# Readout at the end of TensorE's scan step, half of a convolution on VectorE, distances stored by token

## The reference

```
u = silu(conv4(u) + conv_b)                       # causal, 4 taps, per channel, per sequence
dt, B, C = split(u @ W_x.T)
delta = softplus(dt @ W_dt.T + b_dt)
for t in 32 tokens:
    h = exp(delta_t * A) * h + (delta_t * u_t) outer B_t
    y_t = sum over the state of h * C_t
out = ((y + u * Dp) * silu(z)) @ W_out.T
```

## Time and profile before

| | us |
|---|---|
| median of 3 runs | 1948.91 (1948.72 to 1953.33) |
| the profiled execution | 1953.92 |
| its span, first to last instruction | 1952.1 |
| TensorE busy | 1711.4 |
| VectorE busy | 1011.8 |
| ScalarE busy | 761.7 |
| GpSimd busy | 703.1 |

### The profile page before, as it was taken

How to read it: one execution, slowest core, us unless ns; L and a number is a source line. 1 busy time by engine, 2 the same in 40 slices (tenths; PEclk the granted TensorE clock), 3 DMA queues, 4 the chain that set the end, 5 groups by cost and what they waited for, 6 DMA issues and landing times.

```text
span 1952.1 us, 24426 instructions
## 1 busy us (share of the span) xinstructions
PE 1711.4 (88%) x9096; PEld 821.3 (42%) x9096; DVE 1011.8 (52%) x1520; ACT 761.7 (39%) x1201; POOL 703.1 (36%) x430
## 2 busy tenths in 40 slices
PE   7888886898999999999997759999812979899998
PEld 4666663542322332332333525444401557644443
DVE  2444444255888888888884333222359464522121
ACT  1333332196676666666661222111413240112121
POOL 0433330215998998998995010000000014000000
PEclk8999997798999999999999768999865879789999
DMA  2111101002000100100100600111062100101110
GB/s 68 32 32 32 32 27 52 0 8 96 12 12 7 29 12 7 29 12 7 29 6 17 223 1 0 33 48 32 5 143 70 33 0 1 44 1 43 44 43 21
DMA packets 36491, 65.63 MB, mean 34 GB/s; under 512 B 13509, under 2 KB 22617, under 8 KB 34981
## 3 DMA queue, kind: packets, MB, share of 16 engines
q1 hardware_dynamic: 33204, 63.42, 11.0%
q10 hardware_dynamic: 3200, 1.07, 0.2%
HBM read 55.80 MB, written 8.67 MB: 33 GB/s over the span
## 4 chain that ended last, share of the span: by engine, by line
PE 80%; DVE 12%; ACT 2%; DMA 2%; issue 2%; POOL 1%; SPq 1%; DVEq 0%; ACTq 0%; POOLq 0%
PE ps L845 17%; PE ps L888 7%; PE ps L1376 6%; PE ps L2123 6%; PE ps L2112 6%; PE ps L860 5%; PE ps L201 4%; PE ps L1389 3%; PE ps L342 3%; PE ps L347 3%; PE ps L224 3%; PE ps L360 2%; DVE arena L477 2%; PE ps L1887 2%; PE ps L1903 2%
## 5 line engine op out<-in xcount | busy, mean ns | idle before, releaser
L1156 POOL TENSOR_TENSOR arena<-arena 128x768 f32<-128x768 f32 x248 | 521.5, 2122 | 75.2 <-DVE arena L1106 45.0
L845 PE MATMUL ps<-arena 32*128 32x512 f32 x2016 | 368.7, 647 | 2.9 <-DMA arena<-m_bd 2.9
L1106 DVE TENSOR_TENSOR arena<-arena,ps 128x1024 f32<-128x1024 f32 x248 | 302.0, 1218 | 11.7 <-POOL arena L1156 5.5
L845 PEld LDWEIGHTS ps<-arena 32*128 32x128 f32 x2016 | 130.0, 184 | 194.2 <-issue 165.2
L1086 DVE TENSOR_TENSOR arena<-arena,ps 128x1024 f32<-128x1024 f32 x124 | 151.4, 1221 | 87.5 <-PE ps L845 87.5
L1012 ACT ACTIVATE arena<-arena 128x1024 f32<-128x1024 f32 x124 | 131.0, 1057 | 166.1 <-DVE arena L1086 166.1
L2069 POOL TENSOR_TENSOR arena<-arena 128x1024 f32<-128x1024 f32 x16 | 29.9, 1896 | 435.0 <-DVE arena L2002 421.7
L888 PE MATMUL ps<-arena 128*32 128x512 f32 (+15 forms) x1024 | 136.2, 604 | 9.4 <-DVE arena L1106 8.9
L1019 ACT ACTIVATE arena<-ps 128x1024 f32<-128x1024 f32 x124 | 127.0, 1024 | 19.7 <-PE ps L845 3.4
L1021 ACT ACTIVATE arena<-arena 128x1024 f32<-128x1024 f32 x124 | 131.1, 1057 | 3.9
L1376 PE MATMUL ps<-arena 128*128 128x512 f32 x288 | 131.8, 602 | 0.6 <-ACT arena L1441 0.6
(11 more groups left out here) (291 smaller groups left out, 2345.3 us busy)
## 6 DMA issues: line engine op xcount, KB each, us to landing
arena<-ctxT SPq DMA_DIRECT2D x32, 257.0 KB, 3.0
arena<-ctxT SPq DMA_DIRECT2D x8, 1028.0 KB, 15.2
arena<-L_ffn_w SPq DMA_DIRECT2D x16, 512.0 KB, 4.3
arena<-ctx_rows SPq DMA_DIRECT2D x8, 960.0 KB
m_rows<-arena SPq DMA_DIRECT2D x16, 256.0 KB, 3.0
arena<-m_rows SPq DMA_DIRECT2D x64, 64.0 KB
arena<-L_ffn_eW SPq DMA_DIRECT2D x8, 512.0 KB, 3.5
m_yd<-arena SPq DMA_DIRECT2D x64, 32.0 KB, 2.3
```

The costliest lines, as they stand in the source:

```text
L845: mm = nc.tensor.matmul(ps[:, bank + jj, :], weights[r], m_row[r, n // CH % 2, n % CH, :], start=start, stop=True)
L1106: nc.vector.tensor_tensor(m_h[:, u, n % 2], m_xa[:, u, n % 2], ps[:, bank:bank + 2, :], ALU.add).then_inc(S["m_use"], 1)
L1156: nc.gpsimd.tensor_tensor(x, x, m_h[:, u, (n - 1) % 2].rearrange("p j d -> p (j d)")[:, own], ALU.mult).then_inc(S["m_kept"], 1)
```

## The change

1. In the scan, `read_out(n - 1)` comes after `logs(n + 2)`, at the end of the step.
2. The convolution of half 1 is taken from TensorE and done by VectorE from `m_xm` into `m_u` (one product and three fused multiply-adds for each channel block), before the silu. Relu also goes to VectorE (`md_pos`), and the order of TensorE and ScalarE ahead of the scan is new: both `steps_and_b` come before both `step_sizes`, `u_by_token(0)` after them; ScalarE has the silus of both halves together, and its exp of half 1 between the squares of half 0. Banks of the spread of C, of the turned B and of the gate products change.
3. `dist` is laid out (token, segment, 87) in place of (segment, token, 87). The store and the three loads of a group stay one transfer each.

```diff
-        dist = nc.dram_tensor("dist", (3, T, 87), F32, kind="Internal").ap()
+        dist = nc.dram_tensor("dist", (T, 3, 87), F32, kind="Internal").ap()
def conv(h):   # on TensorE
-                    if g == 6:
-                        pe.wait_ge(*S.at("m_eaev", 1))
-                    if g == 7:
-                        pe.wait_ge(*S.at("m_alev", 1))
def steps_and_b(h):
-                pe.wait_ge(*S.at("mc_ev_a", IC * h + IC))
+                pe.wait_ge(*S.at("mc_ev_a", 2 * IC - 1 + h))
def u_by_token(h):
-                    pe.wait_ge(*S.at("md_ev", 2 * q + 2))
+                    pe.wait_ge(*S.at("md_ev", q + 1))
+                    pe.wait_ge(*S.at("md_pos", q + 1))
+                    if h and i < 2:
+                        pe.wait_ge(*S.at("m_cev", 2 * i + 2))
+                    if h and i == 2:
+                        pe.wait_ge(*S.at("m_bev", 2))
...
+            steps_and_b(1)
             step_sizes(0)
-            conv(1)
+            pe.wait_ge(*S.at("m_alev", 1))
+            pe.wait_ge(*S.at("m_eaev", 1))
+            step_sizes(1)
             u_by_token(0)
-            steps_and_b(1)
-            step_sizes(1)
...
             for n in range(8):
-                if n == 0:
-                    pe.wait_ge(*S.at("m_dudone", 4))
-                elif n < 3:
-                    pe.wait_ge(*S.at("m_cev", 2 * n))
-                elif n == 3:
-                    pe.wait_ge(*S.at("m_bev", 2))
+                if n < 4:
+                    pe.wait_ge(*S.at("m_dudone", n + 1))
...
             for n in range(STEPS):
                 drive(n, 0)
-                if n:
-                    read_out(n - 1)
                 if rated(n + 2):
                     rates(n + 2)
                 drive(n, 1)
                 if rated(n + 2):
                     logs(n + 2)
+                if n:
+                    read_out(n - 1)
def parts(h):  # on ScalarE
-                    act.wait_ge(*S.at("md_mm", q + 1))
-                    nc.scalar.activation(m_delta[:, q, :], ps[:, bank_of(h, i), :], ACT.Relu).then_inc(S["md_ev"], 1)
+                    act.wait_ge(*S.at("md_pos", q + 1))
                     nc.scalar.activation(m_e[:, q, :], ps[:, bank_of(h, i), :], ACT.Abs).then_inc(S["md_ev"], 1)
...
             for c in range(IC):
                 convolved(0, c)
+                convolved(1, c)
             steps_and_b(0)
             act.wait_ge(*S.at("m_eat", 1))
             nc.scalar.copy(m_EA, ps[:, 6, :]).then_inc(S["m_eaev"], 1)
+            steps_and_b(1)
             parts(0)
+            exponential(0)
             square(0, 0)
             square(0, 1)
-            convolved(1, 0)
+            parts(1)
             square(0, 2)
-            for c in range(1, IC):
-                convolved(1, c)
             square(0, 3)
+            exponential(1)
             square(0, 4)
-            steps_and_b(1)
-            parts(1)
             square(1, 0)
+            spread_c(0)
             square(1, 1)
-            spread_c(0)
-            square(1, 2)
             spread_c(1)
...
+            square(1, 2)
             square(1, 3)
             square(1, 4)
# on VectorE, after the eight copies
+            for c in range(IC):
+                dve.wait_ge(*S.at("mi_ev_d", IC + c + 1))
+                x3, y3 = (half(v, c, 1).rearrange("p (b t) -> p b t", t=L) for v in (m_xm, m_u))
+                ch.link(nc.vector.tensor_scalar(half(m_u, c, 1), half(m_xm, c, 1), m_cw[:, c, KW - 1:KW], None, ALU.mult))
+                for s in range(1, KW):
+                    ins = nc.vector.scalar_tensor_tensor(out=y3[:, :, s:], in0=x3[:, :, :L - s],
+                                                         scalar=m_cw[:, c, KW - 1 - s:KW - s], in1=y3[:, :, s:],
+                                                         op0=ALU.mult, op1=ALU.add)
+                    if s < KW - 1:
+                        ch.link(ins)
+                ins.then_inc(S["m_dconv"], 1)
# and before the products of softplus
+            for q in range(TT):
+                dve.wait_ge(*S.at("md_mm", q + 1))
+                nc.vector.tensor_scalar(m_delta[:, q, :], ps[:, bank_of(q // 4, q % 4), :], 0.0, None,
+                                        ALU.max).then_inc(S["md_pos"], 1)
# distances
-                    sp.dma_start(d_D[r, k:k + L].rearrange("p j i -> p (j i)"),
-                                 dist[k, g * P:(g + 1) * P].rearrange("(b j) i -> b (j i)", j=L)).then_inc(S["d_back"], 16)
+                    sp.dma_start(d_D[r, k:k + L],
+                                 dist[g * P:(g + 1) * P, k].rearrange("(b j) i -> b j i", j=L)).then_inc(S["d_back"], 16)
-                act.dma_start(dist[:, g * P:(g + 1) * P].rearrange("k p i -> p k i"), d_dt[g]).then_inc(S[f"d_out{g % 4}"], 16)
+                act.dma_start(dist[g * P:(g + 1) * P].rearrange("p k i -> p (k i)"), d_dt[g].rearrange("p k i -> p (k i)")).then_inc(S[f"d_out{g % 4}"], 16)
```

More of the change, by code:

```diff
@@ L798, in m_pe @@
             mm.then_inc(S["m_alt"], 1)
+            steps_and_b(1)
             step_sizes(0)
-            conv(1)
+            pe.wait_ge(*S.at("m_alev", 1))
+            pe.wait_ge(*S.at("m_eaev", 1))
+            step_sizes(1)
             u_by_token(0)
-            steps_and_b(1)
-            step_sizes(1)
             for h in range(NH):
-                pe.wait_ge(*S.at("m_dudone", h + 1))
-                spread_c(h, bank_of(0, h))
-            pe.wait_ge(*S.at("m_dudone", 3))
-            pe.wait_ge(*S.at("m_dtev", 4))
[L809 to L813, removed]
+                pe.wait_ge(*S.at("md_ev", 5 + h))
+                pe.wait_ge(*S.at("md_pos", 5 + h))
+                spread_c(h, bank_of(1, h))
+            pe.wait_ge(*S.at("md_ev", 7))
+            pe.wait_ge(*S.at("md_pos", 7))
+            pe.wait_ge(*S.at("m_dtev", 4))
+            for q in range(TT):
+                mm = nc.tensor.transpose(ps[:, bank_of(1, 2), q * NS:(q + 1) * NS], m_Bc[NS:P, q * P:(q + 1) * P],
+                                         ident[NS:P, NS:P])
+            mm.then_inc(S["m_bmm"], 1)
             u_by_token(1)
             for n in range(8):
-                if n == 0:
-                    pe.wait_ge(*S.at("m_dudone", 4))
-                elif n < 3:
-                    pe.wait_ge(*S.at("m_cev", 2 * n))
-                elif n == 3:
-                    pe.wait_ge(*S.at("m_bev", 2))
+                if n < 4:
+                    pe.wait_ge(*S.at("m_dudone", n + 1))
                 else:
                     pe.wait_ge(*S.at("mz_ev", n - 3))
-                product(bank_of(0, (n + 3) % 4), P, [(m_win[:, k, (IC + n % 4) * P:(IC + n % 4 + 1) * P], half(U[2], k, n // 4))
-                                                     for k in range(DC)], "mz_mm")
+                product(bank_of(0, n % 4), P, [(m_win[:, k, (IC + n % 4) * P:(IC + n % 4 + 1) * P], half(U[2], k, n // 4))
+                                               for k in range(DC)], "mz_mm")
             pe.wait_ge(*S.at("mz_ev", 8))
@@ L931, in convolved @@
                 g = IC * h + c
-                act.wait_ge(*S.at("mc_mm", g + 1))
-                nc.scalar.activation(half(m_u, c, h), ps[:, g, :], ACT.Silu,
+                if h == 0:
+                    act.wait_ge(*S.at("mc_mm", c + 1))
+                    src = ps[:, g, :]
+                else:
+                    act.wait_ge(*S.at("m_dconv", c + 1))
+                    src = half(m_u, c, h)
+                nc.scalar.activation(half(m_u, c, h), src, ACT.Silu,
                                      bias=m_cb1[:, c:c + 1]).then_inc(S["mc_ev_a"], 1)
@@ L1006, in m_act @@
                     act.wait_ge(*S.at("mz_mm", 4 * h + i + 1))
-                    nc.scalar.activation(half(m_z, i, h), ps[:, bank_of(0, (i + 3) % 4), :], ACT.Silu).then_inc(S["mz_ev"], 1)
+                    nc.scalar.activation(half(m_z, i, h), ps[:, bank_of(0, i), :], ACT.Silu).then_inc(S["mz_ev"], 1)
             logged(1)
@@ L1144, in m_pool @@
                 pool.wait_ge(*S.at("m_quad", 5 * h + 5))
-                pool.wait_ge(*S.at("md_ev", 8 * h + 8))
+                pool.wait_ge(*S.at("md_pos", 4 * h + 4))
                 for q in range(4 * h, 4 * h + 4):
```

14 lines of the change are left out of this document (8 added, 6 removed).

## The result

The changed kernel takes **2049.24 us** (median of four, 2047.08 to 2055.82) against 1948.90 for the kernel before in the same comparison: ratio 1.0515, 95% interval 1.0486 to 1.0543, +95 to +106 us. The profiled execution took 2048.51 us (span 2046.7), +94.6 in both against that of before. The forecast was 2028, its range ended at 2046: the sign came out, and so did the mechanism of the largest part, but not the size.

What follows compares the result with a forecast made beforehand. It took the mixer's scan as the bound, its 4.57 us step closing over readout, rates and state u=1, with TensorE nearly full. Scan +81, setup -0.7, distances -1 gave +79: median 2028 us, range 2008 to 2046.

Steps and rivals of the forecast that it cites:

- The first link: Scan step, new order: from d0 to VectorE's start on state u=0, 1.18 us of the predicted 5.25 us step.
- Scan: +81 us: Moved readout: +0.68 us in 123 of 128 steps, less 1 us at each of three crossings between groups.
- TensorE's own sum: Scan step, new order: TensorE's work without the new wait on VectorE, put at 4.94 us.
- The first rival: Scan step: TensorE's own sum of 4.94 us decides, the new wait doesn't; +40, 1989 us; chance 0.08.
- The lost neighbours: Scan step: log spread runs alone (1.07 us), d0 beside rates on the same rows (0.94 us), losing their side-by-side overlap.
- my own sum for the old order without waits: Scan step, old order: TensorE's sequence without waits takes 4.12 of the 4.57 us period.
- the upper bound: Distances by token: the stage's worst case, +10 us, if contention comes on top of the pieces' own cost.

Runs made afterwards that it cites:

- late pause: An unused VectorE reduction behind the wait for d0's result, delaying state u=0: 2104.95 us in the changed kernel, 1957.10 us in the kernel before.

## Why the prediction went wrong

- **Direction and mechanism of part 1: right.** The step closes over state u=0 and the log product's banks, link by link as predicted: 1.23 (1.18 predicted), 1.28 (1.26 to 1.27), 0.75 (0.75), 1.06 (1.07), 0.97 (0.99). TensorE waits 0.53 before the log product (0.3 to 0.5 predicted), the readout never waits, GpSimd idles one microsecond. The late pause shows that the loop that sets the step goes through state u=0. The first link is what was short: 1.18 came from rates with d1 beside them, and d0, with rates next in its own rows, takes 1.23. The step comes to 5.30 in the mean, within my bounds of 5.12 to 5.31, but at their end: +0.736 a step instead of +0.68.
- **Part 1's size: the first of two terms of the sum that failed.** "Scan: +81 us" is the step's +0.68, which was 0.736, and 1 us off for each crossing. The eight steps around an undisturbed crossing went from 35.87 to 40.53, +4.66; seven of them have a log product, 7 x 0.736 = 5.15. So a crossing gives back 0.5, half of what I took. I had read the 2.51 of the earlier trace rows as the time that TensorE stands; it is idle time of the weight loads. The matmuls stand for 1.68 there and for 1.24 at a crossing of the changed kernel (the rows below, before and after). 123 x 0.736 - 3 x 0.5 = 89.0. Measured, the scan is 586.8 us in the mean of the six profiles with the old order and no pause, 675.9 of the three with the new one, **+89.2** where I had +81.

```profile
600.72 1.04 PE L888 MATMUL ps<-arena 128*4 128x512 f32 x8 [1.68 <-DVE arena L1106]
```

```profile
617.49 0.82 PE L859 MATMUL ps<-arena 64*128 64x512 bf16 x6 [1.24 <-DVE arena L1127]
```

- **The estimate of TensorE's own sum**, 4.94, was too high: d0, rates and d1 take 1.99 together and not 0.94 + 1.19. It is 4.76. The first rival had it deciding the step; the late pause shows that it doesn't. The lost neighbours, which I priced from a row at half clock, are the smaller part of the loss against the old period (0.2), the wait the larger (0.53). Against my own sum for the old order without waits, 4.12, which no run tests, they are 0.6; the old period had room for most of that.
- **Part 2: right.** -0.7 predicted, -0.8 in the profiles, no difference in the times; 13.27 us of TensorE's work removed where it wasn't on the path.
- **Part 3: the second term that failed.** "I take -1 us, near the middle of the two, since bytes and engines stay." It is +6.6, between the bounds but near the upper one. That the engines stay was the very reason against it: with only four engines to carry the loads, what counts is what a piece costs there. I priced it at 21 ns, from stores. The loads' 3072 pieces took 36.1 ns in the mean in the changed kernel, 27.7 us on each of the four engines, against 24 x 0.75 = 18.0 before: 9.7 more. (751 ns for each 11136-byte piece, where I had 930; in the other profiles of that layout 605 to 674, so 14.5 to 16.2 us.) Of this 6.6 are left at the end of the wait.
- **The sum.** 89.2 - 0.8 + 6.6 = 95, against 79: the scan's 8 and the distances' 8 are the miss. Each lay inside its own bounds, on the same side, and the range, whose upper end was 2046, left no room for both. The medians differ by 100 (95 to 106). The 5 us between stand in no term, and where they lie stays open; the readout alone shows the like, with +94 in the times for 90 in its scan. That the two profiled executions differ by 94.6 is a coincidence of stretches: before's had the longest wait for the distances of its layout (15.52), and the changed one longer stretches elsewhere.

The Trainium skill (DMA: Bandwidth & Descriptors, How many engines (k)) has the number of engines from the slowest dimension; the trace agrees, with 28.1% of sixteen for four partitions and 98.9% for sixteen. The Trainium skill's Specifications table, on the same page, speaks against pieces under 512 bytes, and by that alone the upper bound would have been the value. The measured +6.6 is nearer to it than my value was, but the same pieces over sixteen engines give a wait of 11.36 us, below that of the long pieces over four (13.1). The two go together: over four engines the short pieces cost 6.6 us, over sixteen 1.2 to 1.9 (11.36 against 10.14 and 9.44). The Trainium skill (TensorEngine Tiling (Array Packing), Key Properties) says that a change of tiling mode drains TensorE. To count such changes and nothing else is out: the three orders with four changes of mode in a step take 4.57, 4.72 and 5.30 us, and the one with three (the readout ahead of the log product) 5.05.

## What to carry to other kernels

When an instruction is moved to the end of a loop, look at what it stood in front of: the time it filled there may have been somebody's wait, and the wait comes back with everything behind it. To learn whether an idle time is slack or path, delay the instruction that ends it, behind its last own wait, in both kernels: 0.46 us gave 0.47 a step in the one and nothing in the other. And before making a transfer's pieces shorter or longer, count the partitions of one transfer: loads of four left most of the sixteen engines out here, and there the short pieces cost most.

## What was not expected of the hardware

- The same DMA instruction, a load of 128 pieces, holds SyncE for 0.60 to 2.1 us in the changed kernel, 1.00 in the mean over the 24, while the engines are at work without a pause. It looks as if SyncE waited for room behind it, and then a longer issue time would be a sign of full engines and not of a costly issue; no run tests this. With loads of 4 long pieces, in the kernel before, an issue takes 0.24 to 0.40.
- The same stretches of code differ by 4 to 6 us from one execution to the next (the first, fourth and last stretch of the table). For one stretch it can be read: the normalization ahead of the distances took 3.2 us more after than before, with a granted clock of 0.50 where before's had 0.72. The rows are windows of the kernel before and of the changed one:

```profile
1390.00:1396.00 6.00, 5.09 (x8) 1.99 (x8) 1.97 (x4) 2.53 (x2) 0.00 (x0) 0.72 0.00 0
```

```profile
1473.70:1479.70 6.00, 5.30 (x7) 2.21 (x8) 1.79 (x3) 2.15 (x2) 0.00 (x0) 0.50 0.00 0
```

  A sum made against one profiled execution carries such differences in it; a difference of two single profiles here says nothing of effects below 5 us, unless it is cut by stage, and even then the distances' wait lay anywhere from 11.49 to 15.52 us in five executions with the same code in that stage.
